# Inverse norms of queries and keys: GpSimd's power and one Newton round in place of a chain on VectorE

## What is computed

```python
x = attn_layer(shift_tokens(x), Wqkv[i], q_scale[i], k_scale[i], Wo[i]) + x
x = ffn_layer(shift_tokens(x), ln_g[i], ln_b[i], W1[i], b1[i], W2[i], b2[i]) + x
```

```python
def l2norm(t):
    return t / jnp.maximum(jnp.linalg.norm(t, axis=-1, keepdims=True), 1e-12)
```

## Time and profile before

| | |
|---|---|
| Runs | 5227.39, 5234.47, 5242.10 us; median 5234.47 |
| Profiled execution | 5226.82 us, of it span 5225.0 |
| Busy DVE | 4421.3 us (85%) |
| Busy PE, ACT, POOL | 3937.0 (75%), 3037.3 (58%), 2558.9 (49%) |

### The profile page before, as it was taken

The page is one execution under the profiler, slowest core; times in us unless marked ns, Lnnn a source line. Parts: engine busy times, 40 slices in busy tenths (PEclk is TensorE's granted clock), DMA queues, the critical chain, the costliest instruction groups (busy, mean ns, idle before and its releaser), DMA issues. The chain is left out here.

```text
span 5225.0 us, 110651 instructions
## 1 busy us (share of the span) xinstructions
PE 3937.0 (75%) x39296; PEld 2895.4 (55%) x39296; DVE 4421.3 (85%) x7733; ACT 3037.3 (58%) x4880; POOL 2558.9 (49%) x1652
## 2 busy tenths in 40 slices
PE   5777777877778777847858677777777777787777
PEld 4655655656646656625535456566466465565565
DVE  8988989979979989845425499799899799899897
ACT  4755756747747647611412467477477476575575
POOL 5645636636636636420010166376366366464562
PEclk8989999989989989977968899899899899999999
DMA  1000000000000000030020000000000000000000
GB/s 46 9 22 12 7 26 8 7 27 7 7 26 8 20 14 8 6 77 11 2 73 1 22 17 7 27 7 7 26 8 21 13 8 20 14 8 22 12 7 12
DMA packets 35925, 88.86 MB, mean 17 GB/s; under 512 B 8209, under 2 KB 14225, under 8 KB 33681
## 3 DMA queue, kind: packets, MB, share of 16 engines
q1 hardware_dynamic: 35568, 84.29, 5.9%
HBM read 38.92 MB, written 1.05 MB: 8 GB/s over the span
## 5 line engine op out<-in xcount | busy, mean ns | idle before, releaser
L770 POOL TENSOR_TENSOR pool<-pool 128x512 f32<-128x512 f32 x768 | 1066.1, 1409 | 969.0 <-DVE pool L868 969.0
L775 POOL TENSOR_TENSOR pool<-pool 128x1024 f32<-128x1024 f32 x384 | 1072.6, 2793 | 171.5 <-DVE pool L879 150.9
L442 PE MATMUL psum<-squares,pool 128*128 128x128 f32 x3072 | 461.2, 297 | 432.1 <-POOL pool L775 272.9
L442 PEld LDWEIGHTS psum<-squares,pool 128*128 128x128 f32 x3072 | 355.1, 149 | 598.8 <-issue 350.6
L879 DVE TENSOR_TENSOR pool<-pool 128x1024 f32<-128x1024 f32 x384 | 678.7, 1806 | 6.7
L482 PE MATMUL psum<-wqkv_hi,xs_lo 128*128 128x512 f32 x1152 | 518.6, 450 | 198.6 <-DVE pool L848 106.2
L645 ACT COPY pool<-psum 64x512 f32<-64x512 f32 x768 | 447.1, 582 | 370.2 <-PE psum L442 364.8
L473 PE MATMUL psum<-pool 128*64 128x128 f32 x6144 | 562.2, 297 | 123.3 <-ACT pool L660 123.3
L419 PE MATMUL psum<-pool 128*128 128x128 f32 x3072 | 451.2, 307 | 130.4 <-ACT pool L645 130.0
L858 DVE TENSOR_REDUCE pool<-pool 128x16 f32<-128x1024 f32 x384 | 449.8, 1210 | 81.9 <-ACT pool L684 81.8
L419 PEld LDWEIGHTS psum<-pool 128*128 128x128 f32 x3072 | 417.1, 217 | 179.7 <-ACT pool L645 168.2
(11 more groups left out here) (162 smaller groups left out, 8291.0 us busy)
## 6 DMA issues: line engine op xcount, KB each, us to landing
pool<-pool SPq DMA_DIRECT2D x192, 128.0 KB, 2.3
pool<-in_wqkv SPq DMA_DIRECT2D x12, 1536.0 KB, 6.0
k_st<-turn_st SPq DMA_DIRECT2D x4, 3072.0 KB, 18.4
pool<-in_wo SPq DMA_DIRECT2D x12, 512.0 KB, 3.6
pool<-in_w SPq DMA_DIRECT2D x12, 341.0 KB, 3.0
k_st<-head_st SPq DMA_DIRECT2D x64, 48.0 KB
q_st<-head_st SPq DMA_DIRECT2D x64, 48.0 KB
pool<-in_w SPq DMA_DIRECT2D x12, 192.0 KB, 2.9
```

Source lines behind the costliest of these rows:

```text
L442: last = pe.transpose(bank(7 - p % 2)[:, P * j:P * j + P], rot[:, p // 2, 2 * c:2 * c + 2, :], ident)
L770: last = g.tensor_tensor(rot[:, q, :, hd * r:hd * r + hd], qn[:, q, :, hd * (1 - r):hd * (2 - r)], tab, ALU.mult)
L775: g.tensor_tensor(rot[:, q], rot[:, q], by_cos[:, q], ALU.add).then_inc(rot_ready, 1)
```

## The change

The sum of squares goes over to GpSimd, which takes its maximum with 1e-24 into `floor` and raises it to the exponent -0.5 into `root`, by a tensor of constants. VectorE goes through the softmax pieces of U-2 without any link in between, waits for `root_ready`, and does one Newton round (three instructions) on it. The result `norm` takes the place of `nwt[3]` in L868. GpSimd's two instructions stand behind `rest(U+1)` and ahead of L770 in its step. The feed-forward part and the layer norms keep their `rsqrt`.

```diff
+        minus_half = sb("minus_half", [P, 2 * HEADS])
...
+                v.memset(minus_half[:], -0.5)
...
-            nwt = [cut(2 * HEADS) for _ in range(4)]
+            floor, root, newt, norm = [cut(2 * HEADS) for _ in range(4)]
...
                             if has(-1):
                                 rest(U + 1, k + 1)
                             if has(0):
+                                g.wait_ge(ss_ready, done(U))
+                                plain(g)
+                                g.wait_ge(norm_step, done(U - 1, 3, 2))
+                                plain(g)
+                                g.tensor_scalar(floor, ss, 1e-24, None, ALU.max).then_inc(ss_held, 1)
+                                g.wait_ge(ss_held, done(U))
+                                plain(g)
+                                g.tensor_tensor(root, floor, minus_half[:], ALU.pow).then_inc(root_ready, 1)
...
-                                last.then_inc(norm_step, 1)
-                                v.wait_ge(norm_step, done(U, RSQRT + 1, 0))
-                                rsqrt(v, ss, nwt, norm_step, done(U, RSQRT + 1, 0), ALU.max, 1e-24, None, None,
-                                      between=probabilities(U - 2) if has(2) else ())
+                                last.then_inc(ss_ready, 1)
+                                if has(2):
+                                    for piece in probabilities(U - 2):
+                                        piece()
+                                v.wait_ge(root_ready, done(U))
+                                v.scalar_tensor_tensor(newt, root, -0.5, floor, ALU.mult, ALU.mult).then_inc(norm_step, 1)
+                                v.wait_ge(norm_step, done(U, 3, 0))
+                                v.tensor_tensor(newt, newt, root, ALU.mult).then_inc(norm_step, 1)
+                                v.wait_ge(norm_step, done(U, 3, 1))
+                                v.scalar_tensor_tensor(norm, newt, 1.5, root, ALU.add, ALU.mult).then_inc(norm_step, 1)
+                                v.wait_ge(norm_step, done(U, 3, 2))
...
-                                                    nwt[3][:, HEADS * q:HEADS * (q + 1)].unsqueeze(2)
+                                                    norm[:, HEADS * q:HEADS * (q + 1)].unsqueeze(2)
```

More of the change, by code:

```diff
@@ L66, in macaron_program @@
         o_ready, o_out, wo_ready, y_ready = sem("o_ready"), sem("o_out"), sem("wo_ready"), sem("y_ready")
+        ss_ready, ss_held, root_ready = sem("ss_ready"), sem("ss_held"), sem("root_ready")
         norm_step, soft_step = sem("norm_step"), sem("soft_step")
@@ L95, in macaron_program @@
             "scalar": [xs_ready, sq_ready, v_out, t_out, p_ready, pt_ready, o_out, fsq_ready, gel_ready],
-            "vector": [qn_ready, cos_ready, s_taken, block_ready, y_ready, norm_step, soft_step,
+            "vector": [ss_ready, qn_ready, cos_ready, s_taken, block_ready, y_ready, norm_step, soft_step,
                        xc_ready, diag_ready, xn_ready, hid_ready, x_ready, var_step, aff_step],
-            "gpsimd": [lo_ready, w_hi, w_split, sin_ready, rot_ready, turn_ready, k_kept],
+            "gpsimd": [ss_held, root_ready, lo_ready, w_hi, w_split, sin_ready, rot_ready, turn_ready, k_kept],
         }
```

## The result

The changed kernel runs in 5954.1 us (median of four runs, 5951.7 to 5958.7), the kernel before in 5233.5. The ratio is 1.1377, with an interval of 1.1357 to 1.1396. The range that was forecast ended at 5500.

A forecast was written before the change was run, and what follows sets the result against it. VectorE's time per attention unit was taken as the bound. Per layer 14 x 0.21 + 1.38 - 1.8 = 2.52 us, times 12 about 30 us, gave 5205 us against the median 5234.5; range 5175 to 5500.

The forecast's parts named there:

- The bound, and E as the gate: Attention loop: VectorE's time per unit (18.13 us) counts; E, the second L775's end, holds back L144 and its replacement.
- Pieces: Eleven softmax pieces on VectorE, called without links in between, taking turns with GpSimd, end at E + 3.70 us.
- Newton and L868: After the pieces, three exposed links take 0.69 us; L868 follows at E + 4.40, 0.21 less per steady unit.
- Start of the power: On GpSimd, after copy, L744 and max, the power begins at about E + 2.15 us.
- Handover: From the power's end on GpSimd to VectorE's Newton round: 0.12 us.
- First units: k = 0 and 1 of a layer, without softmax pieces: 1.47 + p and 2.13 + p us, together gaining 1.38 - 2p.
- p: Time of GpSimd's 128x32 power; taken as 0.9 us, hidden behind the softmax pieces below 1.44 us.
- Price of the power: GpSimd's 128x32 power, in no row: 0.9 us from 20 guessed steps of 0.04 us, range 0.2 to 2.9.
- The other anchor: VectorE's reciprocal costs five times L824 per element; this ratio on GpSimd's 2.13 ns put the power at 0.5 us.
- my own formula: Gain per layer: 14 steady units at 0.21 us, less any power time beyond 1.44, plus 1.38 - 2p; times 12 layers.
- the power outlasts its cover: Rival: VectorE idles before Newton; beyond 1.44 us each extra us costs one in each of 192 units; slower, chance 0.37.
- the forecast case: Power of 0.2 to 1.44 us stays hidden: 5188 to 5218 us, 5205 at 0.9 us; chance 0.41.

The follow-up runs named there:

- the run with the cheap product: The changed kernel with GpSimd's power replaced by an ordinary 128x32 product of two constant tiles, inverse root left out: 5137.5 us, ratio 0.9816 to the kernel before.

## Why the prediction was wrong, step by step

- The bound, and E as the gate: right. In the changed kernel the first L825 of the pieces waits for E as L144 did, and L144's 1.64 us were mainly waiting: alone it takes 0.18.
- Pieces: forecast to end at E + 3.70, measured E + 3.40. The L825 take their turns with copy, L747 and max as forecast; what lay too high is the sum of 0.36 and 0.17 for their holds, 0.53, of which 0.23 were seen: the fourth L825 had next to nothing left to wait for.
- Newton and L868: forecast E + 4.40 with a power that is hidden, measured E + 3.96 in the run with the cheap product. Of the 0.44 us between, 0.30 are the earlier end of the pieces; the other 0.14 are the links and L886, which overlap with what stands ahead of them by more than was taken. The gain per unit was set at 0.21 and is 0.53 by the unit's length; the sign is right and the size too small.
- Start of the power: forecast E + 2.15, measured E + 1.92. Handover forecast 0.12, measured 0.03.
- First units: at k = 1 of the second layer E is 496.30 and L886 starts at 503.85, 7.55 us against 2.13 + p = 7.59: there the formula holds. At k = 0 it does not: from the end of L869 at 475.57 to L886 at 482.97 are 7.40 us against 1.47 + p = 6.93. The max starts 0.45 us after L869 ends, where a handover of 0.1 was taken.
- Price of the power: this is the step that failed. I took 0.9 us and allowed 2.9, from a guessed count of steps and the price of a step in a copy. It is 5.46 us, 160 ns per column, where the copy has 1.2: some 130 such steps, and not 20 or 70. The other anchor, the ratio of VectorE's reciprocal to its transposes, gave 0.5; a ratio of two operations on one engine said nothing about the power on another. The row nearest in name pulled the estimate to the wrong end.

With p = 5.46 my own formula gives 14 x (0.21 - 4.02) + 1.38 - 10.92 = -62.9 us per layer, 755 in all, hence 5989 us; measured is 5954. The mechanism was the rival "the power outlasts its cover", held at 0.37; the forecast case failed nearly by this one term. By the formula the change as a whole pays only while p is below 1.53 us, as 14 x (0.21 - (p - 1.44)) + 1.38 - 2p is nothing there. By the run with the product (cover 1.4, then 0.53 us to lose) it would pay up to some 1.9 us in steady units.

The steps add up: 168 steady units at 3.47 us are 583, and at k = 1 a layer loses 7.55 - 2.15 = 5.4, 65 in all; at k = 0 it loses 7.40 - 2.83 = 4.57, 55 in all. That is 703 of the 720 us. The other 17 are not placed.

The rows for the first two units of the second layer:

```profile
476.02 0.29 POOL L768 TENSOR_SCALAR pool<-pool 128x32 f32<-128x32 f32 x1 [0.74 <-DVE pool L869]
476.50 5.45 POOL L771 TENSOR_TENSOR pool<-pool,minus_half 128x32 f32<-128x32 f32 x1 [0.18 <-POOL pool L768]
493.96 2.34 POOL L786 TENSOR_TENSOR pool<-pool 128x1024 f32<-128x1024 f32 x1
...
482.97 2.36 DVE L886 TENSOR_TENSOR pool<-psum,pool 128x1024 f32<-128x1024 f32 x2 [0.22 <-DVE pool L881]
503.85 2.35 DVE L886 TENSOR_TENSOR pool<-psum,pool 128x1024 f32<-128x1024 f32 x2
```

## What to carry over

Where a whole forecast hangs on one price that no row shows, work out the value at which the sign turns, and widen the range by the ignorance of that price; don't let a row of another engine with a similar name narrow it. An operation whose duration is largely waiting for a shared path is no gain when removed: look at what will stand in its place, and at whether it needs the same path. Work that doesn't need the path is worth most where the other engine holds it, as long as it doesn't bring the next instruction that does need the path in front of the other engine's next one: the sums moved ahead of L144 by themselves gained 0.2%.

## What the runs showed of the hardware

- GpSimd's power in fp32: 160 ns per column. It takes the same 5.4 us for 32 columns on 16, 32 and 128 partitions, and with base 3 and exponent -0.5, with base 1 and with exponent 1. It takes 1.2 us for 4 columns, 20.8 for 128. A sum of 128x32 takes 0.25 us.
- VectorE instructions with two tensors from SBUF, or one-tensor forms such as L144, and GpSimd instructions take turns on a path, one instruction each: in the changed kernel three L825 in a row end 0.28 to 0.29 us behind the end of the GpSimd instruction ahead of them. A GpSimd copy takes its turn too (L815 0.89 us behind it, 0.41 otherwise); a sum on VectorE runs beside it (0.67 us, and 0.68 elsewhere). Whether the first link came 0.06 us ahead of GpSimd's addition or 0.46 us behind it decided 106 us of a kernel's time.
- A link of a dependent chain of 128x32 on VectorE is 0.23 us when exposed. Six links that mostly stood between softmax pieces were worth 121 us: if the 24 first units give 24 x 6 x 0.23 = 33, the other 88 are 0.09 us per link.
